# Preparation of an LSTM kernel's split weights spread anew: a sum formed while Wh arrives, h0 loaded first, float32 products of steps 4 to 7 one gap later

## The reference

```python
xW = einsum('ntd,dg->ntg', x, Wx) + b          # x (32, 512, 512), Wx (512, 2048)
def step((prev_h, prev_c), xw_t):
    a = xw_t + prev_h @ Wh                     # Wh (512, 2048)
    i, f, o = sigmoid(a[:, :H]), sigmoid(a[:, H:2*H]), sigmoid(a[:, 2*H:3*H])
    g = tanh(a[:, 3*H:])
    next_c = f * prev_c + i * g
    next_h = o * tanh(next_c)
out = x + hs                                   # all hidden states, h0 = cond_1024
```

## Time and profile before

| | us |
|---|---|
| median of 3 runs | 2542.74 (2542.69 to 2542.77) |
| the profiled execution | 2543.45 |
| its span, first to last instruction | 2541.4 |
| PE busy in it | 2525.8 (99%) |
| DVE busy | 1938.7 (76%) |
| ACT busy | 1554.5 (61%) |
| mean granted clock of PE | 0.999 |

### The profile page before, as it was taken

How to read it: one execution, slowest core, us unless ns; L and a number is a source line. 1 busy time by engine, 2 the same in 40 slices (tenths; PEclk the granted TensorE clock), 3 DMA queues, 4 the chain that set the end, 5 groups by cost and what they waited for, 6 DMA issues and landing times.

```text
span 2541.4 us, 161390 instructions
## 1 busy us (share of the span) xinstructions
PE 2525.8 (99%) x67268; PEld 1801.8 (71%) x67268; DVE 1938.7 (76%) x8091; ACT 1554.5 (61%) x5895; POOL 160.8 (6%) x264
## 2 busy tenths in 40 slices
PE   9999999999999999999999999999999999999998
PEld 3677777777777777777777777777777777777775
DVE  7777777777777777777777777777777777777776
ACT  8666666666666666666666666666666666666664
POOL 1000000000000000000000000000000000000000
PEclk9999999999999999999999999999999999999999
DMA  7111111111112111111121111111111121111111
GB/s 238 43 37 37 41 45 37 37 41 45 37 37 41 45 37 37 41 45 37 37 41 45 37 37 41 45 37 37 41 45 37 37 42 45 37 37 43 43 33 35
DMA packets 58364, 114.24 MB, mean 45 GB/s; under 512 B 6496, under 2 KB 7136, under 8 KB 57312
## 3 DMA queue, kind: packets, MB, share of 16 engines
q0 software_dynamic: 19008, 35.53, 9.9%
q1 hardware_dynamic: 39248, 78.30, 9.1%
q10 hardware_dynamic: 80, 0.03, 0.0%
HBM read 79.23 MB, written 33.55 MB: 44 GB/s over the span
## 4 chain that ended last, share of the span: by engine, by line
PE 98%; DVE 1%; DMA 1%; ACT 0%; SPq 0%; issue 0%; DVEq 0%; ACTq 0%
PE Z L389 72%; PE run L389 19%; PE extra L389 6%; DMA h_T<-in_h_cols 1%; DVE wx_lo L932 0%; ACT tanh_c L644 0%; DVE h_hi L994 0%; SPq L309 0%; DVE gc L1011 0%; DVE igfc L1005 0%; ACT act L633 0%; ACT wx_hi L658 0%; DVE gc L1020 0%; DVE igfc L1007 0%; DVE hT_hi L999 0%
## 5 line engine op out<-in xcount | busy, mean ns | idle before, releaser
L389 PE MATMUL Z<-wh_hi,hT_hi 128*32 128x512 f16 x8176 | 795.9, 379 | 7.0 <-DVE hT_hi L999 6.9
L389 PE MATMUL Z<-wh_lo,hT_hi 128*32 128x512 f16 x8176 | 796.0, 379 | 0.0
L633 ACT ACTIVATE act<-Z 128x128 f32<-128x128 f32 x1024 | 287.2, 281 | 569.7 <-PE Z L389 569.7
L389 PE MATMUL Z<-wh_hi,hT_lo 128*32 128x512 f16 x8176 | 529.8, 379 | 0.0
L644 ACT ACTIVATE tanh_c<-gc 128x64 f32<-128x64 f32 x1024 | 262.8, 257 | 311.3 <-DVE gc L1020 248.7
L389 PE MATMUL run<-wx_hi,x_hi 128*32 128x256 f16 x6048 | 427.3, 273 | 1.2 <-DVE x_lo L799 1.2
L389 PE MATMUL Z<-wx_hi,x_hi 128*32 128x256 f16 x6048 | 427.4, 273 | 0.2 <-DVE wx_lo L932 0.2
L389 PE MATMUL Z<-wx_lo,x_hi 128*32 128x256 f16 x6048 | 427.3, 273 | 0.0
L389 PE MATMUL Z<-wx_hi,x_lo 128*32 128x256 f16 x6048 | 427.3, 273 | 0.0
L389 PE MATMUL run<-wx_lo,x_hi 128*32 128x256 f16 x6048 | 427.3, 273 | 0.0
L389 PE MATMUL run<-wx_hi,x_lo 128*32 128x256 f16 x6048 | 427.3, 273 | 0.0
(11 more groups left out here) (121 smaller groups left out, 3923.3 us busy)
## 6 DMA issues: line engine op xcount, KB each, us to landing
y<-in_x_rows POOLq DMA_DIRECT2D x127, 256.0 KB, 4.0
out_y<-y SPq DMA_DIRECT2D x127, 256.0 KB, 2.0
x_T<-in_x_cols SPq DMA_DIRECT2D x126, 256.0 KB, 2.7
wx_raw<-in_Wx SPq DMA_DIRECT2D x4, 1024.0 KB, 12.8
wh_raw<-in_Wh SPq DMA_DIRECT2D x4, 1024.0 KB, 13.5
t<-in_Wx SPq DMA_DIRECT2D x3, 512.0 KB, 18.5
t<-in_Wx POOLq DMA_DIRECT2D x3, 512.0 KB, 5.8
x_raw<-in_x_cols SPq DMA_DIRECT2D x2, 256.0 KB, 6.2
```

The costliest lines, as they stand in the source:

```text
L389: return nc.tensor.matmul(out, lhsT, rhs, start=False, stop=last, skip_group_check=True)
L633: nc.scalar.activation(half_gates(act, a)[:, 0:2], half_gates(Z[s], a)[:, 0:2], ACT.Sigmoid, scale=scale).then_inc(gates_done, 1)
```

## The change

- SP loads h0 ahead of Wh. The block for T1's second chunk is loaded after the difference bias, once raw_done, t4_made and the cut of B21 allow it, into the first half of wx_raw's chunk 2 (no longer into t1's second half); POOL adds into the same place.
- T4 for cp = 0 is written to t1's second half, so `make_t4` waits only for T2. DVE makes it before the sums of Wh instead of after them.
- DVE sums the second half of Wh chunk 2 as well as of chunk 3; ACT sums only the first half of chunk 2. ACT cuts T3 (cp = 0) before the sums of Wh chunks 2 and 3.
- `rest_of_raw` no longer makes the bias product. Ahead of step 1 stand the rest of steps 2 and 3 with their biases, and the biases of 4 and 5. The rest of step 4, 5, 6, 7 comes in the gap after step 1, 2, 3, 4; the bias of 6 and 7 in the gap after step 2 and 3.
- ACT cuts T1 (cp = 1) after step 4 with T3, behind scale_raw(7); B22 moves from after step 4 to after step 5.
- DVE cuts T4 (cp = 0) after step 6, ahead of T4 (cp = 1), instead of after step 2.

```diff
--- before.py
+++ after.py
@@ -98,7 +98,7 @@
 
 
 
-        wh_sum = sb("wh_sum", [P, NCH + 1])
+        wh_sum = sb("wh_sum", [P, NCH + 2])
         wx_sum = sb("wx_sum", [P, 2, 4])
         wmax = sb("wmax", [P, 2])
         wmax_all = sb("wmax_all", [P, 2])
@@ -264,6 +264,10 @@
                 return t1[:, 0]
             if cp == 1 and k == W_NAMED["T4"]:
                 return t3[:, 0]
+            if cp == 0 and k == W_NAMED["T4"]:
+                return t1[:, 1]
+            if cp == 1 and k == W_NAMED["T1"]:
+                return w_block(1, 0)[:, 0]
             return (w_block(0, 0), w_block(1, 0), w_block(1, 1), w_block(1, 0), t1, w_block(0, 1), t3)[k][:, cp]
 
 
@@ -345,15 +349,18 @@
             load_raw_x(0)
             load_weights(sp, wx_raw, Wx, wx_loaded, WX_ARRIVE[1:2])
             load_raw_x(1)
+            sp.dma_start(h_T[:, :, :].rearrange("p ch b -> p (ch b)"), h0_cols).then_inc(h0_loaded, 16)
             load_weights(sp, wh_raw, Wh, wh_loaded, range(NCH))
-            sp.dma_start(h_T[:, :, :].rearrange("p ch b -> p (ch b)"), h0_cols).then_inc(h0_loaded, 16)
             sp.dma_start(bias_bc[:, :], bias_rows).then_inc(bias_loaded, 16)
             load_weights(sp, wx_raw, Wx, wx_loaded, WX_ARRIVE[2:])
             load_x(2, 0)
             load_x(3, 1)
             sp.dma_start(t3[:, 1], Wx[3][:, HG:]).then_inc(t3_loaded, 16)
-            sp.dma_start(t1[:, 1], Wx[1][:, HG:]).then_inc(t1_loaded, 16)
             sp.dma_start(bias_d[:, :], bias_rows[:, HW:]).then_inc(bias_d_loaded, 16)
+            sp.wait_ge(raw_done, 2)
+            sp.wait_ge(t4_made, 1)
+            sp.wait_ge(wx_lo_cut, CUT[W_NAMED["B21"], 0] + 1)
+            sp.dma_start(w_form(W_NAMED["T1"], 1), Wx[1][:, HG:]).then_inc(t1_loaded, 16)
             sp.wait_ge(wx_lo_cut, CUT[W_NAMED["T3"], 0] + 1)
             sp.dma_start(t3[:, 0], Wx[3][:, 0:HG]).then_inc(t4_loaded, 16)
             sp.wait_ge(wx_lo_cut, CUT[W_NAMED["T1"], 0] + 1)
@@ -420,7 +427,6 @@
                 return mm
 
             def rest_of_raw(s):
-                bias_part(s)
                 for ch in WX_ARRIVE[2:]:
                     mm = raw_x_part(s, ch)
                 mm.then_inc(raw_summed, 1)
@@ -448,8 +454,11 @@
             for ch in WX_ARRIVE[2:]:
                 mm = raw_x_part(1, ch)
             mm.then_inc(raw_summed, 1)
-            for s in range(2, TB + 1):
+            for s in range(2, TB):
+                bias_part(s)
                 rest_of_raw(s)
+            bias_part(TB)
+            bias_part(TB + 1)
 
             def product(k, q, e, b, col, chunks=(0, 1)):
 
@@ -531,8 +540,10 @@
                             first_recurrent_part(s)
                         else:
                             recurrent_part(t, s)
-                        if isinstance(t, int) and t < TB:
-                            rest_of_raw(TB + t)
+                        if isinstance(t, int) and t <= TB:
+                            rest_of_raw(TB + t - 1)
+                        if isinstance(t, int) and 2 <= t < TB:
+                            bias_part(TB + t)
                     if s % 2 == 0:
                         if taken(q + 1):
                             mm = third_products(q + 1, 1 - e)
@@ -689,9 +700,10 @@
             sum_of_wh(0, G)
             cut_wx_hi(0, "T2")
             sum_of_wh(1, G)
-            sum_of_wh(2, G)
+            cut_wx_hi(0, "T3")
+            sum_of_wh(2, HG)
             sum_of_wh(3, HG)
-            cut_wx_hi(0, "T3", "B22", "T4")
+            cut_wx_hi(0, "B22", "T4")
             sc.wait_ge(w_scale_done, 1)
             cut_wh_hi(0)
             sc.wait_ge(z_done, 1)
@@ -718,13 +730,14 @@
                     cut_wx_hi(1, "T2")
                     scale_raw(5)
                 if s == 3:
-                    cut_wx_hi(1, "B21", "T1")
+                    cut_wx_hi(1, "B21")
                     scale_raw(6)
 
             def last_cuts(s):
                 if s == 0:
-                    cut_wx_hi(1, "T3")
                     scale_raw(7)
+                    cut_wx_hi(1, "T1", "T3")
+                if s == 1:
                     cut_wx_hi(1, "B22")
                 if s == 2:
                     cut_wx_hi(1, "T4")
@@ -872,18 +885,18 @@
                 nc.vector.tensor_reduce(wx_sum[:, cp, 2:3], wx_raw[:, ch, HG:], AX.X, ALU.add,
                                         apply_absolute_value=True).then_inc(wx_summed_2, 1)
 
-            def sum_of_last_wh():
-                v.wait_ge(wh_loaded[3], 16)
-                nc.vector.tensor_reduce(wh_sum[:, 4:5], wh_raw[:, 3, HG:], AX.X, ALU.add,
+            def sum_of_half_wh(ch):
+                v.wait_ge(wh_loaded[ch], 16)
+                nc.vector.tensor_reduce(wh_sum[:, ch + 2:ch + 3], wh_raw[:, ch, HG:], AX.X, ALU.add,
                                         apply_absolute_value=True).then_inc(wh_summed_2, 1)
 
             def largest_weight(k):
 
                 if k == 0:
                     v.wait_ge(wh_summed, NCH)
-                    v.wait_ge(wh_summed_2, 1)
-
-                    nc.vector.tensor_tensor(wh_sum[:, 3:4], wh_sum[:, 3:4], wh_sum[:, 4:5], ALU.add).then_inc(wh_sums_joined, 1)
+                    v.wait_ge(wh_summed_2, 2)
+
+                    nc.vector.tensor_tensor(wh_sum[:, 2:4], wh_sum[:, 2:4], wh_sum[:, 4:6], ALU.add).then_inc(wh_sums_joined, 1)
                     v.wait_ge(wh_sums_joined, 1)
                 else:
                     v.wait_ge(row_max_done, 2)
@@ -920,8 +933,6 @@
 
             def make_t4():
                 v.wait_ge(t2_made, 1)
-                v.wait_ge(raw_done, 2)
-                v.wait_ge(wx_lo_cut, CUT[W_NAMED["B21"], 0] + 1)
                 nc.vector.tensor_tensor(w_form(W_NAMED["T4"], 0), w_block(1, 0)[:, 0], w_form(W_NAMED["T2"], 0),
                                         ALU.add).then_inc(t4_made, 1)
 
@@ -973,8 +984,9 @@
                 cut_wx_lo(0, "B11")
                 make_t2()
                 cut_wx_lo(0, "B21", "T1", "T2")
-                sum_of_last_wh()
                 make_t4()
+                sum_of_half_wh(2)
+                sum_of_half_wh(3)
                 largest_weight(0)
                 cut_wx_lo(0, "T3")
                 weight_scale(0)
@@ -1076,7 +1088,6 @@
                         scale_tables()
                         scale_block(2, 0)
                     if first(n) and s == 2:
-                        cut_wx_lo(0, "T4")
                         cut_wx_lo(1, "B11")
                     if first(n) and s == 3:
                         cut_wx_lo(1, "T2")
@@ -1086,6 +1097,7 @@
                         if s == 1:
                             cut_wx_lo(1, "T3", "B22")
                         if s == 2:
+                            cut_wx_lo(0, "T4")
                             cut_wx_lo(1, "T4")
                     if s == 3 and within(n + 3, NB):
                         field_of_sum(n + 3, 1 - r)
@@ -1143,7 +1155,7 @@
 
             share_wmax(0)
             add_w(t3[:, 1], t3_loaded, Wx[1][:, HG:], t3_added)
-            add_w(t1[:, 1], t1_loaded, Wx[1][:, 0:HG], t1_added)
+            add_w(w_form(W_NAMED["T1"], 1), t1_loaded, Wx[1][:, 0:HG], t1_added)
             add_w(bias_d[:, :], bias_d_loaded, bias_rows[:, 0:HW], bias_d_done)
             add_w(t1[:, 0], t2_loaded, Wx[1][:, 0:HG], t2_added)
             share_wmax(1)
```

## The result

The changed kernel takes **2546.73 us** (median of 20 runs, 2546.01 to 2547.88), the kernel before 2542.74 us (2542.61 to 2543.47, 20 runs): ratio 1.0016, interval 1.001 to 1.0022. It is 4.0 us slower; the forecast was 0.55 us faster, and neither its range (to 2543.6) nor its worst rival (2543.9) holds the result. The profiled execution took 2547.31 us, its span is 2545.2 us where the kernel before had 2541.4.

A forecast was written before the change was run, and what follows sets the result against it. TensorE bounds from 83.07 us on, so only preparation and the first eight steps can gain: 0.35 + 0.75 + 0.1 + 0.55 = 1.75, less 1.2, gives 0.55 us: 2542.74 to 2542.2, range 2541.2 to 2543.6.

The forecast's parts named there:

- what the moved cut of T4 gives back: Step 6's tail on DVE: T4's first low cut costs 1.2 us there, leaving 0.55 us of the 1.75 gained.
- the part on other edits: T1's later load, the B22 cut and added waits: no cost taken, at most 0.2 us for B22, waits under 0.1.
- PE waits for Wh[3]'s low cut before the end of step 1: Last wh_lo products of step 1: PE waits some 0.8 us for the cut ending near 39.5; step 1 0.35 us earlier.
- gap 1 idles, step 2 waits for scale_raw(2): PE between steps 1 and 2: products fall from 2.59 to 1.72 us; idle for ACT's scaling, no loss.
- D(3): Start of step 3's first product on DVE: from 52.60 to 51.45 to 51.5, 0.75 us beyond the earlier 0.35.
- step 5, from 60.07, at full clock: PE's step 5 starts near 58.9 without the clock fall, as float32 products fill the gap before it.
- wait for set_c11 after step 5: PE waits some 1.1 us between step 5 and the second products, hidden in the same chain.
- D(7): Start of step 7's first product on DVE: from 76.61 to near 76.0, after two cuts; 0.55 us earlier.
- rival c: Two stacked T4 cuts idle PE before step 8 and its clock falls there: 1.15 us slower, 2543.9; chance 0.12.
- the two chains that the sum followed: Wh cuts bring step 1's end 0.35 us earlier; DVE's steps add 0.75, 0.1 and 0.55, then lose 1.2.
- The clock term: Slow step 5 gone: 0.55 us counted, DVE's idle before its first product of step 5.
- rival (a): Slow-clock step is an accident of the profiled execution, absent from timed runs: no change, 2542.74; chance 0.22.

The follow-up runs named there:

- the kernel with the right counts: Changed kernel with TensorE's wait thresholds on wx_lo_cut set by the order in which the low cuts are really made: 2542.50 us, ratio to before 0.9998.
- experiment 5: Kernel before with only h0 loaded ahead of Wh: 2542.70 us; also the fastest version (T4's first low cut ahead of Wh's) with h0 behind Wh again: 2541.78 us.
- experiment 6: Kernel before with only the float32 products of steps 4 to 7 one gap later and their biases apart: 2542.80 us, ratio 0.9999.
- experiment 3: Kernel before with only T4's first low cut moved after step 6 and TensorE's counts put right: 2543.37 us, ratio 1.0002.
- experiment 6, taken out: Changed kernel with T4's first low cut ahead of Wh's low cuts, float32 products and biases placed as in the kernel before: 2541.34 us.

## Why the prediction was wrong

**The step that failed** is the part on what the moved cut of T4 gives back. I costed it as 1.2 us on DVE, the engine that it was moved on, and asked which engine had slack there. I didn't ask who counts it. A cut is also one tick of `wx_lo_cut`, and the six cuts that it was moved behind are waited for by their number. For PE each then comes one cut late: 0.81 us where the next cut follows at once (before 68.22), 4.00 us where the next one stands behind a whole step. None of the rivals held that, since all of them were about how long things take. In the part on other edits I did look at waits on this counter, but only at SyncE's; their thresholds (2, 3 and 5) are all reached before T4's turn in either order. PE's wait in `product`, which has every form's number, was the one to be read against the new order.

**What the 4.0 us are made of.** Against the kernel with the right counts (4.2 us by the medians, 4.6 between the two profiled executions), PE starts step 7 at 75.60 instead of 70.60, and step 8 at 82.08 instead of 77.39. PE works at its lower level (1.2 GHz) after the long idle (granted clock 0.51 from 73 to 79 us): the 48 products of step 7 take 4.2 us, from 75.60 to 79.79, instead of 2.6. So PE is 5.0 us late at the start of step 7 and 6.6 at its end (79.79 against 73.19). Of this 1.9 us are covered before step 8: the right-counted kernel idles there for 0.22 and 1.32 us, each behind 0.18 us in which the last matmul drains, and the changed kernel doesn't, since DVE made its two T4 cuts during PE's long wait. 4.7 us are left at step 8, and 4.6 in the spans (2545.2 against 2540.6). The clock's share isn't the same in all executions: 13 of the 20 had a mean of 0.998 and took 2546.47 to 2547.88, seven had 0.999 and took 2546.01 to 2546.51.

**The other terms**, by the first microseconds of the profile after and by the kernel with the right counts:

| step of the forecast | forecast | measured |
|---|---|---|
| PE waits for Wh[3]'s low cut before the end of step 1 | 0.8 us, to 39.5 | 0.62 us, to 39.36 |
| gap 1 idles, step 2 waits for scale_raw(2) | yes | 0.97 us idle, to 42.45; DVE's hT_hi (42.44) ended it, scale_raw(2) was done at 42.39 |
| D(3), from 52.60 | 51.45 to 51.5 | 51.29 |
| step 5, from 60.07, at full clock | 58.9, yes | 58.48, 1.00 |
| wait for set_c11 after step 5 | 1.1 us | 0.98 us |
| idle in gap 6, right counts | 0.8 us | 0.16 + 0.63 us |
| D(7), right counts | 76.0 | 75.82 |
| idle before step 8, right counts | 1.5 us | 0.22 + 1.32 us |
| clock falls there (rival c) | no | no, 1.00 |
| time, right counts | 2542.2 | 2542.50 |

So the two chains that the sum followed, the cuts of Wh and DVE's steps, are right within 0.4 us. In the changed kernel's profile PE wasn't kept waiting by Wx[3]: it began the float32 products later than in the profile before (at 6.87 instead of 6.36 us, so it reached Wh at 20.75, with no idle, where the kernel before started on it at 21.23) and came to Wx[3]'s products at 26.76, without a wait. In other profiles the wait is there (0.55 us in experiment 5, 0.29 us with the cut after step 1).

**The clock term was wrong in kind, not in size.** The half-speed step 5 that the profile showed brought 0.55 us, as much as the whole sum. Its size was right: in the profile at full clock of experiment 6, D(5) is at 64.28 instead of 64.89. But the timed median doesn't hold it: by their mean clock, 20 of 33 executions had no such step. That was rival (a), which I gave 0.22. The sum without it would have been 0, and the right-counted kernel is 0.3 us faster by the medians (the profiled executions, of which the one before has the slow step, lie 0.8 us apart: 2543.45 and 2542.65). So the 2542.50 near the forecast's 2542.2 is in part luck. I had the hint on the page: the profiled execution took 2543.45 us, and no run of the three was over 2542.77.

**The Trainium skill's rule** (TensorE: Matmul & The Clock Gate, Why this matters for your kernels, on single long gaps) did hold where a long gap was: after 4.00 us of idle the mean clock from 75 to 80 us is 0.62. This rule doesn't account for step 5, where no idle was over 1.2 us; there the profiles show the fall in some executions (both of the kernel before, and that of h0 alone) and not in another (experiment 3). What decides it stays open.

## What to carry to other kernels

When an instruction that raises a counting semaphore is moved past others, list everyone who waits on that counter and recompute their thresholds from the new order. Those of the instructions that it was moved behind are then too high: that changes no result and shows only as a wait that ends with an instruction which makes nothing the waiter reads. Its own becomes too low, and that can change results (by the code; no run here does it). In a profile the sign to look for is a releaser other than the one that makes the operand; here both write parts of `wx_lo`, and only the times tell them apart, since B22's cut had ended at 68.2 and the wait ended at 73.06. And where the profiled execution is slower than the median of the timed ones by as much as the effect one hopes for, look for the part of the trace that the median doesn't have, before putting it into a sum.

## What the runs showed of the hardware that I hadn't expected

In both profiles of the kernel before, the granted clock is at its lower level in step 5 (0.50 from 60.5 to 62 us), after idles of 0.72, 1.17 and 1.04 us (1.03 in the second) with work between them. By time and mean clock that happened in 13 of 33 executions of this one kernel on one chip and in 8 of 33 on another. The lengths of the idles alone don't decide it: idles of 1.10 and 0.82 us had the fall behind them in one profile (experiment 6, taken out), and 1.17 and 1.04 us had none in another (experiment 3), though 4 of that kernel's 11 executions show 0.999 and were 0.2 to 0.6 us over the median. In the right-counted kernel 0.63, 0.22 and 1.32 us didn't bring it about in its profile. The slow step 5 cost the kernel before 0.7 us (2543.4 against 2542.7) where PE lost 1.7 us to the clock; that DVE's and ACT's chains cover the rest is the reading of the earlier trace rows, not an experiment.
